# Two conditioned layers on one core: row tiles 4 to 7 also get their residual from TensorE transposes, and the orders of the first 15 steps are rewritten

## The reference

```python
# layer 0, weights by language id
h = relu(x @ W1[id0] + b1[id0])          # 512 -> 128
a = h @ W2[id0] + b2[id0]                # 128 -> 512
z = x + a
n = (z - mean(z)) * rsqrt(var(z) + 1e-5) # over the 512 columns
x = x + n * gamma[id0] + beta[id0]
# layer 1, weights by category id
x = x + (x @ W[id1] + b[id1])            # 512 -> 512
```

## Time and profile before

| | |
|---|---|
| median of 3 runs | 312.26 us (312.13 to 312.66) |
| the profiled execution | 311.37 us |
| its span, first to last instruction | 309.6 us |
| TensorE busy | 302.4 us, 98% |
| VectorE, ScalarE, GpSimd busy | 224.8, 211.0, 220.9 us |
| moved by DMA | 64.34 MB, mean 208 GB/s |

### The profile page before, as it was taken

The page is one execution under the profiler, slowest core; times in us unless marked ns, Lnnn a source line. Parts: engine busy times, 40 slices in busy tenths (PEclk is TensorE's granted clock), DMA queues, the critical chain, the costliest instruction groups (busy, mean ns, idle before and its releaser), DMA issues.

```text
span 309.6 us, 4831 instructions
## 1 busy us (share of the span) xinstructions
PE 302.4 (98%) x1424; PEld 244.1 (79%) x1424; DVE 224.8 (73%) x641; ACT 211.0 (68%) x381; POOL 220.9 (71%) x181
## 2 busy tenths in 40 slices
PE   7989999999999999999999999999999999999995
PEld 7535778788888888888888888888888888888884
DVE  0277999596968879596887969688795977889610
ACT  1149695957896859687596958968596874857431
POOL 0048999499699995999869995999959995631000
PEclk9999999999999999999999999999999999999999
DMA  6969968589976896868857897668867381111122
GB/s 215 346 245 323 318 236 269 163 254 285 271 164 198 252 296 182 234 198 233 264 187 202 227 325 223 137 196 266 286 189 207 125 284 36 68 69 71 68 102 102
DMA packets 40399, 64.34 MB, mean 208 GB/s; under 512 B 6068, under 2 KB 10164, under 8 KB 40372
## 3 DMA queue, kind: packets, MB, share of 16 engines
q1 hardware_dynamic: 38976, 61.41, 64.1%
q10 hardware_dynamic: 1396, 2.62, 2.5%
HBM read 47.24 MB, written 16.78 MB: 207 GB/s over the span
## 4 chain that ended last, share of the span: by engine, by line
PE 91%; DMA 4%; ACT 2%; DVE 1%; issue 1%; SPq 1%; ACTq 0%
PE out_ps L897 54%; PE h_ps L897 15%; PE down_ps L897 13%; PE turn_ps L965 9%; DMA xT<-x_cols 2%; DMA w<-w_all 2%; ACT y L411 1%; SPq L193 1%; DVE turn_ps L605 0%; DVE x1T_lo L612 0%; ACT out_sb L429 0%; ACT hT L393 0%; DVE y L561 0%; ACT w_hi L382 0%; PE out_ps L965 0%
## 5 line engine op out<-in xcount | busy, mean ns | idle before, releaser
L897 PE MATMUL out_ps<-x1T_hi,w_hi 128*128 128x512 f32 x256 | 100.6, 393 | 0.4 <-ACT out_sb L429 0.4
L897 PE MATMUL out_ps<-x1T_lo,w_hi 128*128 128x512 f32 x256 | 99.8, 390 | 0.0
L897 PE MATMUL out_ps<-x1T_hi,w_lo 128*128 128x512 f32 x256 | 99.7, 389 | 0.0
L798 POOL TENSOR_TENSOR xrow<-xrow,b_rows 128x512 f32<-128x512 f32 x60 | 77.3, 1297 | 3.7 <-DMA xrow<-x_rows 3.7
L420 ACT ACTIVATE x1T_hi<-turn_ps,gamma_beta 128x512 fp32r<-128x512 f32 x63 | 42.6, 689 | 40.7 <-DVE turn_ps L605 40.6
L803 POOL TENSOR_TENSOR xT_lo<-xT,xT_hi 128x512 fp32r<-128x512 f32 x48 | 62.1, 1295 | 5.8 <-ACT xT_hi L363 5.8
L605 DVE SCALAR_TENSOR_TENSOR turn_ps<-turn_ps,gamma_beta,xT 128x512 f32<-128x512 f32 x63 | 44.8, 752 | 28.5 <-PE turn_ps L965 27.7
L411 ACT ACTIVATE y<-y,shift,rstd 128x512 f32<-128x512 f32 x64 | 51.4, 816 | 19.3 <-DVE shift L596 18.7
L897 PEld LDWEIGHTS out_ps<-x1T_hi,w_hi 128*128 128x128 f32 x256 | 48.1, 188 | 10.8 <-ACT out_sb L429 0.7
L897 PEld LDWEIGHTS out_ps<-x1T_lo,w_hi 128*128 128x128 f32 x256 | 48.1, 188 | 10.1
L897 PEld LDWEIGHTS out_ps<-x1T_hi,w_lo 128*128 128x128 f32 x256 | 48.1, 188 | 10.0 <-issue 0.2
(11 more groups left out here) (53 smaller groups left out, 362.5 us busy)
## 6 DMA issues: line engine op xcount, KB each, us to landing
out_cols<-out_sb SPq DMA_DIRECT2D x64, 256.0 KB, 2.7
xrow<-x_rows SPq DMA_DIRECT2D x29, 512.0 KB, 6.4
xT<-x_cols SPq DMA_DIRECT2D x28, 512.0 KB, 6.3
w<-w_all SPq DMA_DIRECT2D x8, 1024.0 KB, 7.0
w<-w_all SPq DMA_DIRECT2D x15, 256.0 KB, 4.4
b_rows<-b_all SPq DMA_DIRECT2D x8, 256.0 KB, 7.5
xT<-x_cols ACTq DMA_DIRECT2D x4, 256.0 KB, 3.9
xT<-x_cols ACTq DMA_DIRECT2D x2, 512.0 KB, 6.7
```

The costliest lines, as they stand in the source:

```text
L798: nc.gpsimd.tensor_tensor(xrow[:, i % XR, :], xrow[:, i % XR, :], b2_rows[:, m % 2, :], ALU.add).then_inc(rowbias_done, 1)
L897: mm = nc.tensor.matmul(out, lhsT, rhs, start=first and n == 0, stop=last and n == len(terms) - 1, skip_group_check=unchecked)
```

## The change

`SEEDED` becomes 8. `seed(k)` still fills tiles 0 to 3, and for tiles 4 to 7 `down(i)` issues four transposes of the column tiles 4 to 7 into its bank first and then adds its product to them. VectorE uses `add_bias` for these tiles too. `load_rows(4)` and `load_rows(6)` (512 KB each) and GpSimd's `bias_rows(4)` to `bias_rows(7)` are gone. ScalarE issues the four first column loads, then the ids, then `load_cols(4)` and `load_cols(6)`, all ahead of `relu(0)`. The warm-up products read a tile of ones that VectorE fills (`busy`), and stand as 6 + 3 + 1 around `seed(0)` and `seed(1)` in place of 12 in one go. `load_table()`, which ran one square root ahead of all ScalarE work, now stands behind `normalise(0)`. The rest of each `opening()` is in another order.

```diff
-    SEEDED = BLOCK
+    SEEDED = PER
...
+        busy = sb("busy", [P, P])
...
-            return out_ps[i - 2] if 2 <= i < SEEDED else down_ps[i % 2]
+            return out_ps[i - 2] if 2 <= i < BLOCK else down_ps[i % 2]
...
+            nc.vector.memset(busy[:], 1.0).then_inc(busy_done, 1)
             nc.vector.memset(eps[:], EPS).then_inc(eps_done, 1)
...
-                    nc.tensor.matmul(turn_ps[0][:, :P], ident[:], ident[:], start=True, stop=True)
+                    nc.tensor.matmul(turn_ps[0][:, :P], busy[:], busy[:], start=True, stop=True)
...
-                for i in range(SEEDED):
+                if k == 0:
+                    pe.wait_ge(ident_done, 1)
+                for i in range(BLOCK):
...
-                if i >= SEEDED:
-                    pe.wait_ge(y_done, i - 1 if i >= SEEDED + 2 else i + 1 - SEEDED)
+                if i >= BLOCK:
+                    pe.wait_ge(y_done, i - 1 if i >= BLOCK + 2 else i + 1 - BLOCK)
+                if BLOCK <= i < SEEDED:
+                    for k in range(KC):
+                        nc.tensor.matmul(sum_bank(i)[:, k * P:(k + 1) * P], xT[:, BLOCK + k, rows], ident[:],
+                                         start=k == 0, stop=False, is_transpose=True, skip_group_check=True)
...
                 seed(0)
+                warm_up(3)
+                seed(1)
+                warm_up(1)
                 up(0)
...
-            pe.wait_ge(ident_done, 1)
-            warm_up(12)
+            pe.wait_ge(busy_done, 1)
+            warm_up(6)
```

More of the change, by code:

```diff
@@ L452, in opening @@
                 normalise(3)
-                w_high(0, 1)
-                w1_high(2)
[L455 to L462, removed]
+                w_high(0, 3)
+                x1_high(0)
+                x1_high(1)
+                w2_high(1)
+                relu(2)
+                h_high(2)
+                x1_high(2)
@@ L463, in opening @@
+                x1_high(3)
+                w1_high(2)
                 standard(4)
-                h_high(2)
                 standard(5)
+                standard(6)
                 finish(0)
[L467 to L470, removed]
                 normalise(4)
                 normalise(5)
+                standard(7)
+                x_hi(16)
+                x_hi(17)
                 normalise(6)
+                finish(1)
@@ L474, in opening @@
                 normalise(7)
-                x_hi(17)
+                x1_high(4)
+                x1_high(5)
+                finish(2)
                 x_hi(18)
                 x_hi(19)
-                x1_high(4)
-                x1_high(5)
-                relu(3)
+                w2_high(2)
+                w_high(1, 0)
                 standard(8)
                 standard(9)
-                finish(1)
+                relu(3)
+                standard(10)
                 h_high(3)
-                x1_high(6)
@@ L486, in opening @@
[L486 to L489, removed]
                 standard(11)
                 finish(3)
-                w_high(1, 1)
-                w_high(1, 2)
-                relu(4)
                 normalise(8)
+                x1_high(6)
+                x1_high(7)
                 normalise(9)
                 normalise(10)
+                w_high(1, 1)
+                x_hi(20)
                 normalise(11)
+                finish(4)
@@ L499, in opening @@
+                x1_high(8)
+                w_high(1, 2)
                 w_high(1, 3)
-                h_high(4)
[L501 to L509, removed]
+                standard(12)
+                standard(13)
+                finish(5)
+                x1_high(9)
+                relu(4)
@@ L865, in opening @@
                 w_low(1, 3)
+                w2_low(2)
+                bias_rows(16)
                 bias_rows(17)
                 h_low(4)
-                w2_low(2)
             def step(s):
@@ L1062, in opening @@
                 out_part(6, 3).then_inc(out_done, 1)
+                up(19)
+                out_part(7, 0)
                 turn(10)
                 turn(11)
-                out(7)
+                out_part(7, 1)
+                out_part(7, 2)
+                out_part(7, 3).then_inc(out_done, 1)
             def step(s):
```

273 lines of the change are left out of this document (136 added, 137 removed).

## The result

Before: 312.34 us (median of 6 executions, 312.11 to 312.66). Changed: **316.67 us** (median of 6, 314.63 to 316.96). The ratio is 1.0112 with a 95% interval of 1.0085 to 1.0139: slower by 1.1%, where 0.2% faster was forecast. The six fall into two groups: 314.63 and 314.74 with a mean granted clock of 0.998 to 1.0, and four of 316.60 to 316.96 with 0.994 or 0.995. The profiled one took 314.74.

A forecast was written before the change was run, and what follows sets the result against it. TensorE, busy 302.4 of 309.6 us, was taken as the bound; +1.75 - 0.44 - 1.53 - 0.70 + 0.25 = -0.67 us, so 311.6 on the median of 312.26, 0.2% faster, with 310.6 to 313.0 for 8 in 10.

The forecast's parts named there:

- transposes: 16 added on TensorE for tiles 4 to 7, at 0.109 us each with nothing hiding them: +1.75 us.
- `seed(1)`: Its four transposes move from behind up(3) into the wait ahead of up(0): -0.44 us.
- `up(6)`: Loading column tiles 6 and 7 early removes TensorE's wait ahead of up(6): -1.53 us.
- the late wait: At out_part(6, 0), TensorE no longer waits for finish(4), which ScalarE reaches sooner in the new order: -0.70 us.
- new waits at `turn(0)` and `turn(4)`: Normalisation might end late for these turns; 0.25 us taken for three tight places, W1 included, from 0 to 1.2.
- rival 2: A late category matrix or tight turn(4) hands the gain to a new wait: 312.2 to 312.8; chance 0.17.
- Table loads: Two on ScalarE, ahead of relu(0) and standard(0), both hidden: zero; b1 lands at 8.9, first load ends at 10.2.
- W1, b2 and W2 later: At the head, ScalarE's longer queue shares the engines about 1.5 us more; up to 0.2 us expected for W1's last pieces.
- SyncE's head is unchanged: Argument that SyncE's first loads stay as before, against up(0) starting at most 0.5 us sooner (311.1; chance 0.10).
- Rival 3: TensorE's clock rises only after up(0) starts, so up instructions take 0.86 us, not 0.43; rise at 10.5 gives 313.0; chance 0.13.

The follow-up runs named there:

- g1: f1 without the 16 transposes of column tiles 4 to 7, so part of the sum is left out: 309.15 us, 0.9909 of the kernel before.
- f1: Changed kernel with b1 of sample 2 loaded earlier and column tiles 6 and 7 on SyncE's queue behind W2: 311.16 us, 0.9956 of the kernel before.
- g2: f1 with the square root table load back at ScalarE's head: 310.89 us, 0.9948 of the kernel before.
- g3: f4 with the table load behind normalise(0), as in the changed kernel: 312.05 us, 0.9996 of the kernel before.
- e2: Changed kernel with column tiles 6 and 7 loaded behind relu(0) again: 318.79 us, 1.0144 of the kernel before.
- e1: Changed kernel with the ids' loads put back between the second and third column load: 315.99 us, 1.0098 of the kernel before.
- e3: Changed kernel with b1 of sample 2 loaded ahead of row tiles 14 and 15 on SyncE's queue: 313.02 us, 1.003 of the kernel before.
- e4: Changed kernel with 13 warm-up products in place of 1 ahead of up(0): 315.21 us, 1.008 of the kernel before.
- f3: Kernel before with column tiles 6 and 7 ahead of relu(0) on ScalarE's queue, nothing else: 313.26 us, 1.0026 of the kernel before.
- f2: f1 with 8 warm-up products in place of 1 ahead of up(0): 311.14 us, 0.9958 of the kernel before.
- f4: Kernel before with column tiles 6 and 7 on SyncE's queue ahead of the category matrix: 311.37 us, 0.9971 of the kernel before.
- g4: f4 with its 12 warm-up products on the constant tile that VectorE sets: 310.93 us, 0.9952 of the kernel before.

## Why the prediction was wrong

The sum over the two profiled executions closes. The forecast's terms for transposes, `seed(1)`, `up(6)` and the late wait make -0.92; the head adds 2.04 and the wait for b1 of sample 2 adds 1.9: +3.0 us, which is what the spans differ by (309.6 to 312.6).

**The terms that held.** Transposes +1.75: four take 0.43 us in the trace, which is 1.75 for all; g1's medians give 1.5 to 2.0, its profiled execution less. `up(6)` -1.53: no gap at 18.48. `finish(4)` -0.70: the list of waits has no entry for it. The new waits at `turn(0)` and `turn(4)` (0.25 was put down for them and W1 together): none, but the late head hid them. TensorE came to `turn(0)` at 27.09 and to `turn(4)` at 43.66, where 25.3 and 42.0 had been worked out. f1 came at 25.67 and 42.22 without a wait; g2, whose head is sooner, would come to `turn(4)` at 41.2 and waits until 42.00. So the forecast's 42.0 for the other side fits, and rival 2 is not refuted: a sooner head meets it. Table loads: zero, though for another reason than the one given. b1 of sample 0 landed at about 12.5 and not at 8.9: the 3.9 us of the earlier trace rows are the median of two loads, of which this one took 4.9, and it takes 7.5 here. ScalarE's timeline:

```profile
12.51 1.28 ACT L393 ACT_TABLE_LOAD   x1 [12.51 <-DMA b<-b_cols]
```

The load ended at 13.8, behind the end of `up(3)`; `up(4)` and the seeds covered it. g3 shows the 0.8 to 0.9 us that it costs without this cover.

**The step that failed first: "W1, b2 and W2 later ... I expect up to 0.2 there", and with it "SyncE's head is unchanged".** SyncE's head had in fact changed: b1's load is issued at 4.97 in place of 6.07, gamma's and beta's at 5.99 in place of 11.26, b2's at 7.44 in place of 5.01; f1 keeps this and isn't hurt. The term that failed is the 1.5 us for which ScalarE's longer queue shares the engines, put at 0.2 us of TensorE's time; the head lost 2.04. Two things go into it, a lower rate and an uneven share. First the rate. DMA packets of 6 to 7 us with the share of each queue (q10 is ScalarE's, q1 SyncE's), before, and then changed (its first line is shown at e2):

```profile
DMA packets 204, 0.28 MB, mean 281 GB/s; under 512 B 15, under 2 KB 84, under 8 KB 204
...
q10 hardware_dynamic: 126, 0.25, 80.4%
q1 hardware_dynamic: 78, 0.04, 12.1%
```

```profile
q10 hardware_dynamic: 48, 0.08, 36.7%
q1 hardware_dynamic: 118, 0.05, 19.6%
```

The engines are busy for 56% of their time in place of 92, while both queues have work (both move packets until 12 us). From 5 to 8 us 0.53 MB are moved in place of 0.91, on ScalarE's queue 0.41 in place of 0.75 and on SyncE's, which has W1, 0.12 in place of 0.16.

Then the share. From 8 to 10 us both kernels are at the full rate again, 355 and 356 GB/s. Changed, and then SyncE's queue before (ScalarE's is in the earlier trace rows):

```profile
q10 hardware_dynamic: 312, 0.61, 84.7%
q1 hardware_dynamic: 266, 0.10, 19.3%
```

```profile
q1 hardware_dynamic: 591, 0.68, 102.4%
```

W1's queue gets 0.10 MB where it got 0.68, because ScalarE's still has the second pair to move. The trace of before had this to see: SyncE's queue moved 0.04, 0.05, 0.04 and 0.07 MB in the four microseconds from 4 to 8, beside ScalarE's, and 0.32 in the next, when ScalarE's had nearly run dry. So in effect W1 waits for most of what ScalarE's queue holds. As an estimate, the 0.38 MB that the dip left over are 1.1 us at 355 GB/s and the pair's own 0.52 MB are 1.5, together 2.6, of which the head shows 2.04; no run separates the two.

The start of the transposes behind `up(3)` sorts the traces. In the five with both pairs on ScalarE's queue ahead of `relu(0)` (changed, e1, e3, e4, f3) it is 13.18 to 15.04; in the nine without (before, e2, f1, f2, f4, g1, g2, g3, g4) 10.56 to 13.89. Where the clock fell in the head (e1, f3, e2, g4) 1.7 us of it are the clock's; with them taken off it is 13.0 to 13.3 against 10.6 to 12.2. The bytes of 5 to 8 us sort them too, 0.53 to 0.61 MB in the five and 0.70 to 0.97 in the nine. f3 and f4 show it in the time, with nothing else of the change in the kernel. That the second pair at this place is the cause is shown. Why the engines start fewer packets from 5 to 8 us is not; f1 has such a dip too (171 GB/s at 6 to 7 us), over by 7 us, and g4's W1 was late without the second pair. The head varies from one execution to another: it differs by 1.3 us between f1 and g1, which have the same one, and this would account for the kernel before at 311.4 to 314.4 on the same chip.

**The step that is missing: b1 of sample 2.** The diff moves `load_b1(2)` on SyncE's queue behind two loads of rows and `load_cols(20)` and `load_cols(22)`, from 49.45 to 61.65 us, and I did not follow that queue past the head. The part on the late wait followed ScalarE's list up to `finish(4)` and stopped there. `relu(4)` was eight entries on, and its operand was being moved by 12 us. e3 shows it: 2.0 us.

**Rival 3 had the right engine at the wrong moment.** The clock did not rise late. From 4.48 six warm-up instructions take 0.67 us and the four transposes of `seed(1)` 0.44, so 0.11 each, where the first twelve warm-ups take 2.72, 0.23 each: 2.4 GHz already, with the transposes of `seed(0)` among the work that led up to it. In the traces of e1, e3 and f2 `seed(1)` starts at 5.92 and its four instructions step at about 0.21, so there the rise came later, with the same instructions ahead of it, but still ahead of `up(0)`; f3's 24 warm-ups, with no transpose among them, step at 0.22 to their end at 6.81. So the Trainium skill (TensorE: Matmul & The Clock Gate, PE-mode transpose), by which transposes do not engage the full clock, finds no support in these traces: the transposes themselves step at 0.11 once the clock is up. That they count for nothing towards the rise can't be refuted here, since warm-ups stood on both sides. What happened is a fall. W1 is late, TensorE stands idle for 3 us, and 4 of 6 executions have a clock share of 0.994 or 0.995, which in the traces of e1, f3 and g4 is one stretch at 1.2 GHz behind the gap; none of the four has a trace of its own. The price is 2.0 us between the groups (316.7 against 314.7). e4, with the gap filled, has none in five, which fits but is few. It looks like a result of the late W1 and not a third cause: f1 has none in twelve without more warm-ups.

**Outside the span.** Every kernel of the changed order takes 2.1 us beside its span, the kernel before and its variants 1.8. The forecast carried 1.77 over. The table's place (g2 2.1, g3 1.8) and the new tile (g4 1.8) are not it; where the 0.3 us come from stays open.

**The median.** 3.0 in the span, 0.35 outside, 2.05 for the clock that the median execution lost, less 1.0 by which the profiled execution of before lay under its median: 4.4 against the 4.3 measured. This is only the measured times taken apart, and no test of the causes. And what the change was worth without its two faults: f1 at -1.2 us, of which f4 has 1.0 with one line moved in the old order.

## What to carry to other kernels

Bytes over a rate is no model for a load that must land within the first ten microseconds: here the urgent queue got 0.02 to 0.07 MB in a microsecond until the other was nearly done, and the rate itself halved for one or two. So look at the bytes of each queue, microsecond by microsecond, before a load is put beside an urgent one. A load that isn't wanted before 17 us did well behind the urgent ones on their own queue and badly beside them. When a list of DMAs is ordered anew, take each load's first reader and check it, the smallest first: 0.5 KB cost as much as the whole head. A term that a late head hides isn't refuted: once the head is mended, look for the waits it covered. A wait of TensorE near the start costs more than its length if the clock falls after it; look at the clock share of each execution, not only of the profiled one.

## What the hardware showed that was not expected

- Two queues with work on both moved 131 GB/s for a microsecond (before: 281), with the DMA engines idle for 44% of it.
- With both at work, SyncE's queue got 0.10 MB of 0.71 from 8 to 10 us; alone it got 0.68.
- A load of 0.5 KB, issued at 61.65, took 5.9 us behind column and row tiles on its queue; b1 of sample 0 took 4.9 us in the head of before and 7.5 in the changed one.
- With 3 us of idle time ahead of `up(0)`, the clock fell to 1.2 GHz in 4 of 6 executions and not in 2, with the same program (by their clock shares); a fall cost 1.7 us in e1's trace and 2.0 us between the groups.
- The transposes of `seed(1)` step at 0.21 us ahead of the clock's rise (e1's trace) and at 0.11 behind it (the changed kernel's).
